# Macaron block on one core: the router's weight travels with the sorted row, GpSimd adds the gathered rows to x

## The chip, the core and the metric

The kernel runs on 1 core of a Trainium2 chip. The metric is the device time of one execution in microseconds. The engines are named as the profile names them: PE (TensorE, matmuls), PEld (its weight loads), DVE (VectorE), ACT (ScalarE), POOL (GpSimd), SP (SyncE, which only issues DMAs here). Each has its own instruction queue and runs it strictly in order; semaphores tie them together.

## The reference

x is 8 batches of 512 tokens by 256 features, f32. Three residual stages:

```python
x = x + 0.5 * ffn(layernorm(x))
x = x + attn(layernorm(x))
x = x + 0.5 * ffn(layernorm(x))
# ffn: probs = softmax(x @ gate_w.T) over 2 experts; sel = argmax; top_w = probs[sel]
#      h = silu(x @ w_gate[sel].T) * (x @ w_up[sel].T); out = top_w * (h @ w_down[sel].T), 1024 wide
# attn: rms_norm, 16 heads of 16, causal softmax, @ Wo, + its own input
```

With two experts the weight of the chosen one is 1 / (1 + exp(-|logit difference|)).

## The kernel before

The FFN is sparse: only the chosen expert is computed for a token. An *item* is one batch of one of the two FFN stages (16 items). The items are grouped into 12 *passes* of one or two items. For an item the kernel takes a layer norm (`l_stats` DVE, `l_rstd` POOL, `l_norm` ACT), splits the normed f32 rows into an f16 high part (`l_split` on ACT, L698, tile xs) and an f16 low part (`l_split` on POOL, L596), takes the logit difference with w_diff (`l_dlogit`, DVE, L881, four reductions, then three small instructions L889 to L892), finds each token's place in the sorted order with small matmuls (`l_prefix`, PE, L1082), writes the place (`l_pos`, DVE, L903), the weight (`l_coef`, DVE, L911 and L912, tile coef), and scatters the rows to DRAM with four indirect DMAs (`l_scatter`, POOL, L609). SP loads them back transposed (`l_load`, L510, tile x_t). A pass then runs 5 or 9 slots of 128 sorted tokens in two units each: gate and up matmuls (L1118 to L1120), `tanh` ACT, `hid` DVE (L926, L930), `h_split` (ACT L717, POOL L650 makes h_lo), down matmuls (L1137 to L1139), `y_out` ACT (L723), `y_store` to y_sorted. `y_gather` (POOL, L623, four indirect DMAs) brings an item's rows back in token order into yt, and `x_update` (DVE, L918, four instructions of 128x256) does x = x + coef * yt.

Between the FFN work runs the attention: 32 *parts* (8 batches, 4 groups of 4 heads), each with scores (PE L1180, L1182; `row_min` on DVE, L983 to L993), the row maximum split into three f16 rows (`max_parts`, DVE, L1003 to L1007) that travel PE, ACT, SP, DRAM and back into extra contraction rows of qt, transposed scores (PE L1197, L1199), exp twice (ACT L786, L787), the low part of the probabilities (`p_lo`, DVE L1012, every fifth one POOL L655), and the product with v (PE L1217). The norm ahead of attention starts with `stats` on DVE (L937), which waits for the batch's x_update.

One list sets the order of everything: `master()` gives every stage a point on one time axis (about 1.2 us a point in the attention stages), sorts by it, and each engine walks the sorted list and issues the stages that concern it. So a stage's number decides what stands in front of it on its engine's queue. Three banks of PSUM (ps_w) go round among scores, transposed scores, projections and transposes: PE can be at most three such tiles ahead of DVE and ACT. `stats` of batch 2 stands one point behind its x_update; for batch 0 also; for the others the distance is 23 points or more.

Of the kernel before, what the change touches and what calls it, by code (L numbers as in the profile page):

```python
# [19 lines left out]
T = S // P  # L20
# [7 lines left out]
MAX_ROWS = 3  # L28
# [100 lines left out]
EXP_LAG = 0.0  # L129
GATHER_LAG = 8  # L130
# [3 lines left out]
               ("l_split", 0, 6.0), ("l_dlogit", 0, 6.5), ("l_exp", 0, 10.5), ("l_prefix", 0, 11.0),  # L134
# [3 lines left out]
            ("l_split", 0): -59.6, ("l_dlogit", 0): -56.5, ("l_exp", 0): -56.4, ("l_prefix", 0): -55.9,  # L138
            ("l_pos", 0): -55.8, ("l_coef", 0): 20, ("l_scatter", 0): -55, ("l_load", 0): -54}
# [101 lines left out]
def macaron(nc, x, rms_w, gate_w, w_gate, w_up, w_down, w_attn, out):  # L241
    with ExitStack() as ctx:  # L242
# [87 lines left out]
        coef = [sb(f"coef{n}", [P, T], F32) for n in range(ROUTES)]  # L330
# [24 lines left out]
        x_sorted = [nc.dram_tensor(f"x_sorted{n}", [PLACES, 2 * D], F16, kind="Internal").ap() for n in range(2)]  # L355
# [120 lines left out]
        def _(sp):  # L476
# [19 lines left out]
            for st in order:  # L496
# [8 lines left out]
                elif what == "l_load":  # L505
# [50 lines left out]
        def _(pool):  # L556
            link = Links(pool, pool_link)
            pool.memset(yt[0][:, 0, :], 0.0).then_inc(zero_ready, 1)
# [22 lines left out]
            for st in order:  # L581
# [11 lines left out]
                elif what == "l_split":  # L593
# [672 lines left out]
```

## Time and profile before

| | us |
|---|---|
| runs: median (lowest to highest, 3 runs) | 1288.9 (1286.12 to 1292.99) |
| the profiled execution's own time | 1289.34 |
| its span, first to last instruction | 1287.6 |
| PE busy | 1091.3 |
| DVE busy | 905.7 |
| ACT busy | 740.2 |
| POOL busy | 531.7 |
| mean granted clock of TensorE | 0.951 |

A busy engine may still wait in places; the share of busy time is a mean over stages. "Idle before" is the time the engine stood still ahead of an instruction, and the releaser named is what ended it.

### The profile page before, as it was taken

The page shows a single profiled execution, that of the slowest core. Times are in us where ns is not written, and L with a number is a line of the kernel's source. Part 1 is how long each engine was busy: PE and PEld are TensorE (multiplying, and loading weights), DVE is VectorE, ACT ScalarE, POOL GpSimd, SP SyncE. Part 2 cuts the span into 40 slices and gives each one's busy share as a digit, 9 for nine tenths or more (in the row PEclk, how much of TensorE's full clock was granted, in tenths as well). Part 3 has the DMA queues.
Part 4 walks back from the last instruction along what each step waited for, and adds up shares of the span by engine and source line. Part 5 has one row for each costly group of instructions (what it writes and reads, how often), then busy time and mean ns, then how long its engine had stood idle before and what let it go on. Part 6 is the DMA issues. An engine that isn't in the chain of part 4 may idle for free. (4 is left out here: it accounts for less than half of the span.)

```text
span 1287.6 us, 39268 instructions
## 1 busy us (share of the span) xinstructions
PE 1091.3 (85%) x14566; PEld 945.8 (73%) x14566; DVE 905.7 (70%) x1912; ACT 740.2 (57%) x1285; POOL 531.7 (41%) x664
## 2 busy tenths in 40 slices
PE   0686888978989898888898799997999989798895
PEld 0576777857778787777777688976877878688784
DVE  6653548796878886978868877887777877874432
ACT  4432425656657665666666566775766756675321
POOL 3146543254523444445234534244452344444432
PEclk9889899998999999999989899998999989998998
DMA  8203231213211122022122141111321012211111
GB/s 315 69 26 83 75 95 49 64 51 80 62 54 34 38 64 87 22 71 76 60 63 73 39 113 44 31 54 41 85 76 57 28 49 61 74 48 47 51 42 46
DMA packets 101326, 83.54 MB, mean 65 GB/s; under 512 B 50240, under 2 KB 95040, under 8 KB 101152
## 3 DMA queue, kind: packets, MB, share of 16 engines
q1 hardware_dynamic: 84064, 54.29, 14.7%
q0 software_dynamic: 6144, 16.79, 4.2%
q10 hardware_dynamic: 10944, 9.97, 2.3%
q8 instruction: 131, 2.15, 0.7%
q14 instruction: 43, 0.35, 0.1%
HBM read 37.36 MB, written 33.69 MB: 55 GB/s over the span
## 5 line engine op out<-in xcount | busy, mean ns | idle before, releaser
L650 POOL TENSOR_TENSOR h_lo<-hid,h_hi 128x256 bf16<-128x256 f32 x304 | 222.5, 753 | 505.1 <-ACT h_hi L717 504.9
L786 ACT ACTIVATE area<-ps_w,s_scale 128x512 f32<-128x512 f32 x320 | 219.6, 686 | 246.6 <-PE ps_w L1199 188.9
L1118 PE MATMUL ps_g<-x_t,w 128*128 128x128 f16 x1096 | 211.8, 227 | 14.9 <-issue 11.4
L787 ACT ACTIVATE area<-ps_w,s_scale 128x512 f16<-128x512 f32 x320 | 217.9, 681 | 0.0
L1120 PE MATMUL ps_g<-x_t,w 128*128 128x128 f16 x1096 | 212.0, 227 | 2.7 <-issue 2.6
L1119 PE MATMUL ps_g<-x_t,w 128*128 128x128 f16 x1096 | 211.2, 226 | 1.9 <-issue 1.9
L1120 PE MATMUL ps_u<-x_t,w 128*128 128x128 f16 x1096 | 210.3, 225 | 1.8 <-issue 1.8
L1118 PE MATMUL ps_u<-x_t,w 128*128 128x128 f16 x1096 | 210.1, 225 | 1.8 <-issue 1.5
L1119 PE MATMUL ps_u<-x_t,w 128*128 128x128 f16 x1096 | 209.2, 224 | 2.4 <-issue 2.3
L1012 DVE TENSOR_TENSOR area<-area 128x512 f16<-128x512 f32 x256 | 193.3, 756 | 14.8 <-ACT area L787 11.1
L1137 PE MATMUL ps_y<-wd,h_hi 128*128 (+1 forms) x608 | 170.8, 281 | 13.7 <-POOL h_lo L650 11.6
L1138 PE MATMUL ps_y<-wd,h_hi 128*128 (+1 forms) x608 | 170.8, 281 | 1.1 <-issue 1.1
L1139 PE MATMUL ps_y<-wd,h_lo 128*128 (+1 forms) x608 | 170.9, 281 | 0.3 <-issue 0.3
L1197 PE MATMUL ps_w<-qt,kt 68*128 68x512 f16 (+3 forms) x512 | 137.3, 306 | 35.6 <-DVE row_min L988 19.0
L1180 PE MATMUL ps_w<-kt,qt 65*128 65x512 f16 (+3 forms) x512 | 138.2, 308 | 13.5 <-DVE row_min L986 8.2
L1118 PEld LDWEIGHTS ps_g<-x_t,w 128*128 (+1 forms) x1096 | 111.2, 101 | 31.7 <-issue 16.8
L711 ACT ACTIVATE hid<-ps_g,g_scale 128x512 f32<-128x512 f32 x137 | 94.2, 688 | 67.1 <-PE ps_g L1120 46.7
L1217 PEld LDWEIGHTS ps_v<-v_parts,area 128*128 128x128 f16 x2560 | 100.7, 97 | 38.7 <-POOL area L655 11.3
L1217 PE MATMUL ps_v<-v_parts,area 128*128 128x33 f16 x2560 | 115.3, 178 | 14.7 <-POOL area L655 10.0
L926 DVE SCALAR_TENSOR_TENSOR hid<-hid,ps_g 128x512 f32<-128x512 f32 x137 | 93.0, 679 | 40.2 <-ACT hid L711 40.0
L717 ACT ACTIVATE h_hi<-hid 128x512 f16<-128x512 f32 x152 | 95.5, 628 | 42.9 <-DVE hid L930 40.1
L1118 PEld LDWEIGHTS ps_u<-x_t,w 128*128 (+1 forms) x1096 | 109.9, 100 | 13.9 <-issue 3.5
(160 smaller groups left out, 2820.0 us busy)
## 6 DMA issues: line engine op xcount, KB each, us to landing
y_sorted<-ys ACTq DMA_DIRECT2D x76, 128.0 KB, 1.7
qk_scratch<-area SPq DMA_DIRECT2D x32, 256.0 KB, 2.2
qt<-qk_scratch SPq DMA_DIRECT2D x128, 64.0 KB, 2.6
kt<-qk_scratch SPq DMA_DIRECT2D x128, 64.0 KB, 2.6
x_buf<-x SPq DMA_DIRECT2D x8, 512.0 KB, 4.2
out<-x_buf SPq DMA_DIRECT2D x8, 512.0 KB, 3.0
x_sorted<-yt SPq DMA_DIRECT2D x18, 128.0 KB, 1.9
area<-w_down SPq DMA_DIRECT2D x4, 512.0 KB, 12.3
```

What stands on the lines that cost most here:

```text
L650: pool.tensor_tensor(h_lo[:, u % 2, c], hid[:, u % 2, c], h_hi[:, u % 2, c], ALU.subtract).then_inc(h_lo_done, 1)
L786: act.activation(p_f32[:, f % 3], ps[:], ACT.Exp, scale=s_scale[:])
L787: act.activation(p_hi[:, f % 4], ps[:], ACT.Exp, scale=s_scale[:]).then_inc(exp_done, 1)
L1012: dve.tensor_tensor(p_lo[:, f % 4], p_f32[:, f % 3], p_hi[:, f % 4], ALU.subtract).then_inc(lo_done, 1)
L1118: pe.matmul(cols, w_hi, x_hi, start=kb == 0 and f == 0, stop=False, skip_group_check=True)
L1119: pe.matmul(cols, w_hi, x_lo, start=False, stop=False, skip_group_check=True)
L1120: ins = pe.matmul(cols, gate_up(u, kind, 1, kb, q * QF + f), x_hi, start=False, stop=kb == KB - 1, skip_group_check=True)
L1137: pe.matmul(ps_y[:, 0:D], hi, wd_lo, start=q == 0 and f == 0, stop=False, skip_group_check=True)
L1138: pe.matmul(ps_y[:, 0:D], hi, wd_hi, start=False, stop=False, skip_group_check=True)
L1139: ins = pe.matmul(ps_y[:, 0:D], lo, wd_hi, start=False, stop=q == 1 and f == QF - 1, skip_group_check=True)
L1180: pe.matmul(ps[:, at:at + keys], qt[0:MAX_AT_ROW, h, i * P:keys], kt[0:MAX_AT_ROW, h, 0:keys], start=n == 0, stop=False, skip_group_check= ...
L1217: ins = pe.matmul(ps_o[n // KINDS % 2][:, hh, i, :], part[:, n % 4, at + (i - j) * P:at + (i - j + 1) * P], v_parts[b % 2][:, j, h, :], st ...
```

## The change

1. The router's weight is no longer applied at x_update. `l_coef` (DVE) writes 1 / (1 + exp) as a 257th column beside the two f16 halves of each row (tile xs_rows, rows of 272 f32, 1088 bytes in place of 1024). The scatter carries it, and so now waits for `l_coef`; `l_coef` of the next item waits for the scatter. SP loads the column back in sorted order after each transposed load (coef_in: 128 x 5 or 128 x 9 elements of 4 bytes), a small POOL instruction per pass multiplies it by the weights' scale (`coef`), and `y_out` on ACT uses it as its per-row scale.
2. `x_update` moves from DVE (four instructions) to POOL (one of 128x1024: x = yt + x).
3. The low part of the rows gets a stage of its own, `l_low`, at point 8.5 of the routing in place of 6.0; `l_dlogit` moves from 6.5 to 6.0.
4. At the start `l_coef` of the first item moves from point 20 to -55.7, `l_dlogit` from -56.5 to -57.5.
5. The row maximum is split into two f16 rows in place of three: two DVE instructions a part in place of four.
6. The first gather no longer waits for the zeroing DMAs, which read a tile of their own.

```diff
-MAX_ROWS = 3
+MAX_ROWS = 2
...
-               ("l_split", 0, 6.0), ("l_dlogit", 0, 6.5), ("l_exp", 0, 10.5), ("l_prefix", 0, 11.0),
+               ("l_split", 0, 6.0), ("l_dlogit", 0, 6.0), ("l_low", 0, 8.5), ("l_exp", 0, 10.5), ("l_prefix", 0, 11.0),
                ("l_pos", 0, 11.2), ("l_coef", 0, 13.0), ("l_scatter", 0, 14.5), ("l_load", 0, 19.0)]
...
         if s == 0 and q == 1:
             put(p, "flags", n)
+            put(p + COEF_LAG, "coef", n)
...
-        xs = sb("xs", [P, T, 2, D], F16)
+        xs_rows = sb("xs_rows", [P, T, XW], F32)
+        xs = xs_rows[:, :, 0:D].bitcast(F16).rearrange("p i (a d) -> p i a d", a=2)
+        xs_coef = xs_rows[:, :, D:D + 1]
...
-        x_sorted = [nc.dram_tensor(f"x_sorted{n}", [PLACES, 2 * D], F16, kind="Internal").ap() for n in range(2)]
+        x_sorted = [nc.dram_tensor(f"x_sorted{n}", [PLACES, XW], F32, kind="Internal").ap() for n in range(2)]
...
+                    if n >= 2:
+                        sp.wait_ge(coef_done, n - 1)
+                    sp.dma_start(coef_in[n % 2][:, 0:SLOTS[n]].unsqueeze(2), x_sorted[n % 2][
+                        0:P * SLOTS[n], D:D + 1].rearrange("(s p) c -> p s c", p=P),
+                        allow_slow_non_contiguous=True).then_inc(coef_loaded[n % 2], 16)
...
-                elif what == "l_split":
+                elif what == "l_low":
                     n = st[1]
                     pool.wait_ge(l_hi, n + 1)
                     pool.tensor_tensor(xs[:, :, 1, :], xn_f[:], xs[:, :, 0, :], ALU.subtract).then_inc(l_lo, 1)
...
                     pool.wait_ge(l_lo, n + 1)
+                    pool.wait_ge(l_coef, n + 1)
...
-                            xs[:, i].rearrange("p a d -> p (a d)"), None).then_inc(scattered, 16)
+                            xs_rows[:, i, :], None).then_inc(scattered, 16)
+                elif what == "x_update":
+                    n = st[1]
+                    b = ITEMS[n][3]
+                    pool.wait_ge(gathered[n % 2], 64 * (n // 2 + 1))
+                    pool.tensor_tensor(x_of(b)[:], yt[n % 2][:], x_of(b)[:], ALU.add).then_inc(x_updated, 1)
+                elif what == "coef":
+                    n = st[1]
+                    pool.wait_ge(coef_loaded[n % 2], 16 * (n // 2 + 1))
...
+                    pool.tensor_scalar(coef[n % 2][:, 0:SLOTS[n]], coef_in[n % 2][:, 0:SLOTS[n]], y_inv[:], None,
+                                       ALU.mult).then_inc(coef_done, 1)
...
-                    act.activation(ys[g % 2][:], ps_y[:, 0:D], ACT.Copy).then_inc(y_copied, 1)
+                    n, s, _ = UNITS[2 * g]
+                    act.wait_ge(coef_done, n + 1)
+                    act.activation(ys[g % 2][:], ps_y[:, 0:D], ACT.Copy, scale=coef[n % 2][:, s:s + 1]).then_inc(y_copied, 1)
...
-                    link(dve.tensor_scalar(prob[:], e_abs[:], 1.0, y_scale[:], ALU.add, ALU.mult))
-                    link(dve.reciprocal(coef[r][:], prob[:]))
-                elif what == "x_update":
...
-                    for i in range(T):
-                        ins = dve.scalar_tensor_tensor(out=x_of(b)[:, i, :], in0=yt[n % 2][:, i, :],
-                                                       scalar=coef[n % ROUTES][:, i:i + 1], in1=x_of(b)[:, i, :],
-                                                       op0=ALU.mult, op1=ALU.add)
-                    ins.then_inc(x_updated, 1)
+                    if n:
+                        dve.wait_ge(scattered, 64 * n)
+                    link(dve.tensor_scalar(prob[:], e_abs[:], 1.0, None, ALU.add))
+                    dve.reciprocal(xs_coef, prob[:].unsqueeze(2)).then_inc(l_coef, 1)
...
                     link(dve.tensor_scalar(part[0], minima, -1.0 / MAX_SCALE, None, ALU.mult))
-                    link(dve.scalar_tensor_tensor(out=max_rest[:], in0=minima, scalar=-1.0 / MAX_SCALE, in1=part[0],
-                                                  op0=ALU.mult, op1=ALU.subtract))
-                    link(dve.tensor_copy(part[1], max_rest[:]))
-                    dve.tensor_tensor(part[2], max_rest[:], part[1],
-                                      ALU.subtract).then_inc(max_parts_done, 1)
+                    dve.scalar_tensor_tensor(out=part[1], in0=minima, scalar=-1.0 / MAX_SCALE, in1=part[0],
+                                             op0=ALU.mult, op1=ALU.subtract).then_inc(max_parts_done, 1)
```


POOL, the routing of an item at 436 to 444 us in the trace before (xs and xs_rows are the low part, area is p_lo). Before:

```order
L592 TENSOR_TENSOR l_shift<-l_scale,l_minus_mean 128x4
L655 TENSOR_TENSOR area<-area 128x512
L650 TENSOR_TENSOR h_lo<-hid,h_hi 128x256 x2
L596 TENSOR_TENSOR xs<-xn_f,xs 128x4x256
L650 TENSOR_TENSOR h_lo<-hid,h_hi 128x256 x2
L655 TENSOR_TENSOR area<-area 128x512
L650 TENSOR_TENSOR h_lo<-hid,h_hi 128x256 x2
```

After:

```order
L606 TENSOR_TENSOR l_shift<-l_scale,l_minus_mean 128x4
L681 TENSOR_TENSOR area<-area 128x512
L676 TENSOR_TENSOR h_lo<-hid,h_hi 128x256 x4
L610 TENSOR_TENSOR xs_rows<-xn_f,xs_rows 128x4x256
L681 TENSOR_TENSOR area<-area 128x512
L676 TENSOR_TENSOR h_lo<-hid,h_hi 128x256 x2
```

The low part stands behind two more h_lo instructions.

POOL, the gathers and updates of batches 2 and 3 (yt and x_buf; tmp_pool is the first instruction of `rstd`, behind `stats`). Before:

```order
L623 DMA yt<-y_sorted,place 128x256 x4
L650 TENSOR_TENSOR h_lo<-hid,h_hi 128x256 x2
L623 DMA yt<-y_sorted,place 128x256 x4
L655 TENSOR_TENSOR area<-area 128x512
L631 TENSOR_SCALAR tmp_pool<-mean_var 128x4
```

After:

```order
L649 DMA yt<-y_sorted,place 128x256 x4
L676 TENSOR_TENSOR h_lo<-hid,h_hi 128x256 x2
L649 DMA yt<-y_sorted,place 128x256 x4
L681 TENSOR_TENSOR area<-area 128x512
L631 TENSOR_TENSOR x_buf<-yt,x_buf 128x1024
L657 TENSOR_SCALAR tmp_pool<-mean_var 128x4
```

The update of batch 2 stands behind the gather of batch 3 and a p_lo.

DVE at the start, from the logit difference to the placing of the first item. Before:

```order
L881 ISA dlogit 128x1
L889 TENSOR_SCALAR sel<-dlogit 128x4
L890 SCALAR_TENSOR_TENSOR high_place<-dlogit,from_top 128x4
L892 SCALAR_TENSOR_TENSOR neg_abs<-dlogit 128x4
L801 TENSOR_REDUCE w_max<-qt 128x1
L903 TENSOR_TENSOR place<-high_place,ps_w 128x4
L905 CAST low_count<-ps_w 1x1
L801 TENSOR_REDUCE w_max<-kt 128x1 x4
```

After:

```order
L909 ISA dlogit 128x1
L917 TENSOR_SCALAR sel<-dlogit 128x4
L918 SCALAR_TENSOR_TENSOR high_place<-dlogit,from_top 128x4
L920 SCALAR_TENSOR_TENSOR neg_abs<-dlogit 128x4
L829 TENSOR_REDUCE w_max<-qt 128x1 x2
L931 TENSOR_TENSOR place<-high_place,ps_w 128x4
L933 CAST low_count<-ps_w 1x1
L940 TENSOR_SCALAR prob<-e_abs 128x4
L941 RECIPROCAL xs_rows<-prob 128x4
L829 TENSOR_REDUCE w_max<-kt 128x1 x4
```

One more reduction of the weights (w_max) stands ahead of place, and prob and the reciprocal, for which the scatter now waits, right behind low_count.

## Rows read from the trace of the kernel before

**Rows 1.** the page, its span and the busy time of each engine

```profile
span 1287.6 us, 39268 instructions
PE 1091.3 (85%) x14566; PEld 945.8 (73%) x14566; DVE 905.7 (70%) x1912; ACT 740.2 (57%) x1285; POOL 531.7 (41%) x664
```

**Rows 2.** windows view, attention stages; columns: stretch, length, busy of each, PEclk, DMA, GB/s

```profile
190.00:1180.00 990.00, 881.51 (x12079) 761.34 (x12080) 769.20 (x1614) 640.14 (x1121) 410.50 (x495) 0.96 0.20 58
```

**Rows 3.** timeline of PE: start, length, instruction, [idle before and its releaser]

```profile
446.44 0.40 PE L1197 MATMUL ps_w<-qt,kt 68*128 68x256 f16 x1 [3.76 <-DVE row_min L988]
...
1205.14 0.17 PE L1082 MATMUL ps_w<-sel,upper 128*128 128x5 bf16 x1 [1.97 <-DVE neg_abs L892]
```

**Rows 4.** timeline of DVE and POOL before the first of these gaps

```profile
441.10 0.42 DVE L881 CUSTOM_DVE_ANT_0 junk<-xn_f,w_diff 128x256 bf16<-128x256 f32 x1
...
441.57 2.27 DVE L881 CUSTOM_DVE_ANT_0 junk<-xn_f,w_diff 128x256 bf16<-128x256 f32 x1
...
445.70 0.69 DVE L988 TENSOR_REDUCE row_min<-ps_w 128x4 f32<-128x512 f32 x1
...
441.43 2.13 POOL L596 TENSOR_TENSOR xs<-xn_f,xs 128x1024 f16<-128x1024 f32 x1 [1.96 <-ACT xs L698]
```

**Rows 5.** windows view around the first of these gaps

```profile
444.00:446.00 2.00, 0.00 (x0) 0.00 (x0) 1.97 (x7) 0.00 (x0) 0.99 (x2) 0.69 0.42 114
446.00:448.00 2.00, 1.56 (x13) 1.44 (x14) 2.00 (x4) 0.70 (x2) 0.00 (x0) 0.50 0.18 51
```

**Rows 6.** timeline of DVE at another item, 271 us

```profile
270.97 2.09 DVE L1012 TENSOR_TENSOR area<-area 128x512 f16<-128x512 f32 x1
```

**Rows 7.** groups of instructions: line, count, busy us, mean ns, idle before

```profile
L918 DVE SCALAR_TENSOR_TENSOR x_buf<-yt,coef,x_buf 128x256 f32<-128x256 f32 x64 | 30.4, 536 | 17.6 <-DMA yt<-y_sorted,place 17.6
L1006 DVE CAST max_parts<-max_rest 128x16 f16<-128x16 f32 x32 | 9.6, 301 | 1.1
L1007 DVE TENSOR_TENSOR max_parts<-max_rest,max_parts 128x16 f16<-128x16 f32 x32 | 6.5, 204 | 1.1
L596 POOL TENSOR_TENSOR xs<-xn_f,xs 128x1024 f16<-128x1024 f32 x16 | 35.8, 2239 | 32.4 <-ACT xs L698 32.4
```

**Rows 8.** windows view, 10 us stretches with DVE nearly full and PE not

```profile
270.00:280.00 10.00, 6.35 (x87) 5.00 (x84) 9.83 (x25) 5.87 (x11) 4.20 (x5) 1.00 0.04 14
...
1120.00:1130.00 10.00, 6.28 (x80) 5.62 (x78) 9.09 (x21) 5.71 (x11) 4.38 (x5) 0.87 0.01 3
```

**Rows 9.** timelines of POOL, DVE and PE, the update of batch 2 and its norm

```profile
348.70 1.17 POOL L655 TENSOR_TENSOR area<-area 128x512 f16<-128x512 f32 x1
...
348.94 0.75 DVE L937 BATCH_NORM_STATS2 bn<-x_buf 128x6 f32<-128x256 f32 x2
...
350.34 0.23 PE L1180 MATMUL ps_w<-kt,qt 65*128 65x128 f16 x1 [1.75 <-DVE row_min L986]
```

**Rows 10.** timelines of DVE, POOL, SP and PE, the first routing at the start

```profile
17.39 1.21 DVE L801 TENSOR_REDUCE w_max<-qt 128x1 f32<-128x1024 f32 x1
...
19.03 1.23 POOL L609 DMA_INDIRECT x_sorted<-xs,place  x1 [2.65 <-DVE low_count L905]
...
29.18 2.78 SPq L510 DMA_TRANSPOSE x_t<-x_sorted  x1
...
34.10 0.27 PE L1118 MATMUL ps_g<-x_t,w 128*128 128x128 f16 x1 [8.62 <-issue]
```

**Rows 11.** timeline of PE, a wait behind four scatters on POOL

```profile
556.98 0.29 PE L1217 MATMUL ps_v<-v_parts,area 128*128 128x33 f16 x5 [3.48 <-POOL area L655]
```

**Rows 12.** the chain that ended last, its end: start, length, what

```profile
1282.13 0.48 DVE x_buf L918
...
1283.01 0.79 DVE x_buf L918 x2
```

**Rows 13.** the page, DMA queues: packets, MB, share of 16 engines

```profile
q1 hardware_dynamic: 84064, 54.29, 14.7%
q0 software_dynamic: 6144, 16.79, 4.2%
```

More of the change, by code:

```diff
@@ L59 @@
 XSCALE = 2.0**11
+XW = D + 16
 H_SCALE = 2.0**-54
@@ L129 @@
 EXP_LAG = 0.0
+COEF_LAG = 1.0
 GATHER_LAG = 8
@@ L133 @@
 ROUTE_STEPS = [("l_stats", 0, 0.0), ("l_stats", 1, 0.5), ("l_rstd", 0, 1.5), ("l_norm", 0, 4.0),
-               ("l_split", 0, 6.0), ("l_dlogit", 0, 6.5), ("l_exp", 0, 10.5), ("l_prefix", 0, 11.0),
+               ("l_split", 0, 6.0), ("l_dlogit", 0, 6.0), ("l_low", 0, 8.5), ("l_exp", 0, 10.5), ("l_prefix", 0, 11.0),
                ("l_pos", 0, 11.2), ("l_coef", 0, 13.0), ("l_scatter", 0, 14.5), ("l_load", 0, 19.0)]
 START_AT = {("l_stats", 0): -60, ("l_stats", 1): -59.9, ("l_rstd", 0): -59.8, ("l_norm", 0): -59.7,
-            ("l_split", 0): -59.6, ("l_dlogit", 0): -56.5, ("l_exp", 0): -56.4, ("l_prefix", 0): -55.9,
-            ("l_pos", 0): -55.8, ("l_coef", 0): 20, ("l_scatter", 0): -55, ("l_load", 0): -54}
+            ("l_split", 0): -59.6, ("l_dlogit", 0): -57.5, ("l_low", 0): -56.5, ("l_exp", 0): -56.4, ("l_prefix", 0): -55.9,
+            ("l_pos", 0): -55.8, ("l_coef", 0): -55.7, ("l_scatter", 0): -55, ("l_load", 0): -54}
 MAX_AT = [-59, -58, -57, -56, -55, -54, -53, -52, -51.2, -51, -46.8, -46.6]
@@ L267, in macaron @@
         yt = [sb(f"yt{n}", [P, T, D], F32) for n in range(2)]
+        zeros = sb("zeros", [P, XW], F32)
         xt_hi = sb("xt_hi", [P, KB, S], F32R)
@@ L329, in macaron @@
         place = [sb(f"place{n}", [P, T], I32) for n in range(ROUTES)]
-        coef = [sb(f"coef{n}", [P, T], F32) for n in range(ROUTES)]
+        coef_in = [sb(f"coef_in{n}", [P, MAX_SLOTS], F32) for n in range(2)]
+        coef = [sb(f"coef{n}", [P, MAX_SLOTS], F32) for n in range(2)]
         low_count = [sb(f"low_count{n}", [1, 1], I32) for n in range(3)]
@@ L382, in macaron @@
         down_done, y_copied, x_updated = sem("down_done"), sem("y_copied"), sem("x_updated")
+        l_coef, coef_loaded, coef_done, y_inv_done = sem("l_coef"), sems("coef_loaded", 2), sem("coef_done"), sem("y_inv_done")
         proj_done, part1_done, part2_done = sem("proj_done"), sem("part1_done"), sem("part2_done")
@@ L618, in _ @@
                         pool.wait_ge(x_updated, n - 1)
-                    elif n == 0:
-                        for parity in range(2):
-                            pool.wait_ge(zeroed[parity], 16 * MAX_SLOTS)
                     for i in range(T):
@@ L1001, in _ @@
                     minima = row_min[:, p % 2, :, 0, :]
-                    part = [max_parts[:, r].rearrange("p (h i) -> p h i", i=T) for r in range(3)]
+                    part = [max_parts[:, r].rearrange("p (h i) -> p h i", i=T) for r in range(MAX_ROWS)]
                     link(dve.tensor_scalar(part[0], minima, -1.0 / MAX_SCALE, None, ALU.mult))
-                    link(dve.scalar_tensor_tensor(out=max_rest[:], in0=minima, scalar=-1.0 / MAX_SCALE, in1=part[0],
-                                                  op0=ALU.mult, op1=ALU.subtract))
-                    link(dve.tensor_copy(part[1], max_rest[:]))
-                    dve.tensor_tensor(part[2], max_rest[:], part[1],
-                                      ALU.subtract).then_inc(max_parts_done, 1)
+                    dve.scalar_tensor_tensor(out=part[1], in0=minima, scalar=-1.0 / MAX_SCALE, in1=part[0],
+                                             op0=ALU.mult, op1=ALU.subtract).then_inc(max_parts_done, 1)
                 elif what == "p_lo" and st[2] % KINDS < KINDS - 1:
```

22 lines of the change are left out of this document (11 added, 11 removed).

## The prediction, made before the changed kernel ran

> **What bounds the kernel now.** I read the page's busy times first: PE 1091.3 us of a span of 1287.6 [rows 1]. So PE is the bound on the whole, and an instruction taken from another engine is worth something only where PE stands still for it. The windows view of the attention stages (190 to 1180 us) says how much that is at most: PE 881.5 of 990 us, so 108 us idle, at a granted clock of 0.96, while DVE is busy 769.2 us and POOL 410.5 us [rows 2]. Then I went through the timeline of PE for its gaps. The long ones have one pattern. At 446.44 us PE has waited 3.76 us for a row_min of DVE [rows 3]. DVE was late because one of the four reductions of `l_dlogit` took 2.27 us where its neighbour took 0.42 us; it started at 441.57, and POOL had started the low part of the rows (L596, 2.13 us) at 441.43 and held it until that ended [rows 4]. Five gaps of 3.3 to 4.2 us inside the attention stages and one of 1.97 us at 1205 us stand behind such a pair, 20.7 us together (the first and the last of the six are shown) [rows 3]. Each long one costs again behind itself: the granted clock of TensorE falls to 0.69 in the stretch of the gap and is 0.50 (1.2 GHz in place of 2.4) in the next, where PE works again [rows 5]. At items where the low part misses `l_dlogit`, it holds a p_lo of DVE instead: 2.09 us for one L1012 [rows 6].
>
> **A: the low part moves from point 6.0 to 8.5, the logit difference from 6.5 to 6.0.** The low part then stands behind two more h_lo on POOL, some 3 us later, when the reductions are over. At each of the six places DVE gets 2.27 - 0.42 = 1.85 us back [rows 4]. It doesn't keep all: the low part still takes 2.13 us, and while DVE is saturated some L1012 will run into it, up to 2.09 - 0.68 = 1.4 us, where 0.68 is the plain length of the row_min beside it (0.69 in [rows 4]; L1012 has the same shape). I take half of that, 0.7 us. So 6 x 1.15 = 6.9 us. Bounds: 0 (every collision only moves) and 6 x 1.85 = 11.1 us. If gaps of nearly 4 us become gaps of 2, less of the half-clock time follows. One such tail costs about 2 us (2 us at 0.50 shown, about twice that long each time); for five long gaps I take half, 5 us; bounds 0 and 10.
>
> **B: two DVE instructions fewer in `max_parts`.** 9.6 + 6.5 + 2.2 us of idle between them = 18.3 us of DVE over 32 parts [rows 7].
>
> **C: x_update leaves DVE.** It frees 30.4 us [rows 7], and puts 16 POOL instructions of 128x1024 in its place. No row shows this add; the nearest is the low part of the same length, 2.239 us mean [rows 7] and 2.13 us unhindered [rows 4]. I take 2.13, with 1.67 (what DVE takes for it [rows 12]) and twice 2.13 as ends, since both inputs are now f32. Each reads SBUF beside p_lo on DVE, so it can hold an L1012 as the low part does: up to 1.4 us, or nothing. For 13 updates inside the attention stages at the upper end that is 18 us given back, so B and C free 31 to 49 us of DVE, say 36.
> How much of B and C reaches PE? Of the 99 stretches of 10 us between 190 and 1180 us, 14 have DVE at 9.0 us or more and PE below 10 (the first and the last are shown) [rows 8]. Elsewhere freed DVE time is hidden by PE itself. 36 x 14/99 = 5.1 us; bounds 0 and a third, 12 us.
> The trace gives the collision first: a DVE instruction that reads two tiles in SBUF waits out a POOL tensor_tensor [rows 4, 6], while the hid and row_min instructions, which read PSUM, don't show it.
> The Trainium skill says the same of it in "SBUF — State Buffer", section "Who interferes with whom": DVE and GpSimd share a pair of ports by an exclusive lock, and the second one to issue blocks fully, also for a DVE instruction with two SBUF inputs against a GpSimd read. By that rule this change hands DVE 16 more locks, and a saturated DVE would gain nothing from C; this is what the rival "the collisions only move" is made of. "GPSIMD Engine Reference", section "Elementwise — side-by-side cycle accounting", has 4497 ns for an f32 add of 2048 columns; an estimate from it is 2.25 us for 1024, and no row here shows this add.
>
> **D: costs.**
> Start: place now stands behind one more w_max (1.21 us at 17.39), and prob and the reciprocal (about 0.4 us) behind it, ahead of the scatter that starts at 19.03; the reductions start some 0.4 us earlier. From there the chain is scatter, transposed load at 29.18, first gate matmul at 34.10 [rows 10]. The DMA engines are full of weights then, which may hide it. +1.2 us, bounds 0 and +1.7.
> Batch 2: `stats` starts at 348.94 on DVE, but POOL is at its gather and p_lo until 348.70 + 1.17 = 349.87, and only then comes the update: 352.0 [rows 9]. `stats` waits 3.1 us, and row_min, for which PE already stood 1.75 us [rows 9], waits behind it. The 1.7 us that DVE no longer spends just before are mostly lost to waiting. +2.5 us, bounds 0 and +5.
> POOL queue: after the double passes (4 times) the update stands right behind four gather DMAs, with h_lo and p_lo behind it. PE has waited 3.48 us for a p_lo behind four scatters [rows 11], so there is no slack there. Between +0 and 4 x 2.13 = 8.5 us; I take +1.2, as only a p_lo or h_lo due in just that stretch counts.
> End: the last update is on the chain that ends last, 1282.13 to 1283.80 us on DVE, 1.67 us [rows 12]; on POOL 2.13: +0.5.
> At nothing I cost: `y_out` with a scale per row (0 to +0.1 us each, ACT has slack); the scatter's wait for l_coef later on (l_coef stands 1.5 points ahead); 6% longer rows; the smaller row maximum on PE, ACT and SP; the 12 loads of coef_in, 9728 elements of 4 bytes. For these no row exists. By the mean of a packet, 14.7% x 16 x 1287.6 / 84064 = 36 ns on q1 and 4.2% x 16 x 1287.6 / 6144 = 141 ns on q0 [rows 13], the 72 per engine of the largest load take 2.6 to 10 us. They are wanted some 20 points after they are issued, but the row maximum's two DMAs stand behind them on SP's queue.
>
> **Sum.** -6.9 - 5 - 5.1 + 1.2 + 2.5 + 1.2 + 0.5 = -11.6. On the profiled execution's 1289.34 us (its span 1287.6 and 1.7 around it; the median of the runs, 1288.9, is within 0.4 of it) this gives 1277.7, so 1278 us.
>
> **Rivals.**
> *The collisions only move.* The low part and the update catch an L1012 each time, at 1.4 us; A gives 0 and the clock still falls, and B and C together give 5.1 against costs of 5.4: 1289 - 1290 us. For it: rows 6, and that POOL always finds a saturated DVE at these places. Against it: the worst gaps are those where `l_dlogit` was hit, not an L1012.
> *POOL's queue becomes what PE waits for.* Place: each gather of an attention item, then the wait for its landing, then the update, with p_lo and h_lo behind. From the point where a p_lo is due within 2 us after the update starts, PE pays 2.13 us. At 12 items 25.6 us less the gains of 17: 1289.3 + 5.4 + 25.6 - 17 = 1303 if all pay, 1297 at three quarters. For it: rows 11. Against it: POOL is busy 410 of 990 us, and the update stands 8 points, about 10 us, behind its gather, by when most gathers have landed.
> *The small loads hold up the row maximum.* If a coef_in load takes 10 us, the row maximum's round trip behind it on SP and the DMA rings is late at the six passes where it follows within 6 points: about 3 us each with nothing else lost, 18 us: 1296 us.
> *The gaps go altogether.* 1.85 us at six places, all 10 us of slow clock, 12 of B and C: -33 + 5: about 1262.
>
> **Chances.** Forecast (1271 to 1284) 0.48; collisions only move 0.23; POOL's queue 0.14; small loads 0.05; the gaps go 0.10. What a measurement can tell from no change is about 0.5%, 6.4 us. Faster by more than that: 0.43 of the forecast and all of the last, 0.53; within: 0.05 and 0.22, 0.27; slower: 0.14 + 0.05 + 0.01 = 0.20. The cases have both signs, so the range reaches from 1264 to 1297; the forecast's own is 1271 to 1284.
>
> **What would show it.** A: the longest reduction of `l_dlogit` near 0.42 us, PE's gaps behind it near 2 us, the clock above 0.5 there. Collisions moved: L1012 with a higher mean and as many of 2 us. B: max_parts two rows shorter. C: the POOL add at 2.1 us; `stats` of batch 2 waiting for POOL by 3 us. Start: the first gate matmul 1 us later. POOL rival: PE waiting for h_lo or area of POOL by 20 us more in total. Small loads: coef_in landing late and PE waiting for max_scratch. The forecast is wrong if PE's idle time inside 190 to 1180 us doesn't fall by at least 5 us, or its clock there not rise.

## The result, and the profile after

| | before | after |
|---|---|---|
| median, us (lowest to highest, 4 runs each) | 1290.45 (1286.12 to 1292.99) | 1255.34 (1253.81 to 1261.15) |
| ratio, 95% interval | | 0.974, 0.9697 to 0.9782 |
| span of the profiled execution | 1287.6 | 1254.2 |
| PE busy / not busy in the span | 1091.3 / 196.3 | 1078.9 / 175.3 |
| DVE, POOL busy | 905.7, 531.7 | 860.2, 571.8 |
| mean granted clock | 0.951 | 0.963 |

The change is faster by 2.6%, 35 us of medians. I had forecast 1278 us with a range down to 1264, so the sign was right and the size was a third of the measured one. Of the 33.4 us between the two spans 21.0 are idle time of PE. The other 12.4 are busy time for the same number of matmuls (14566), with the mean granted clock at 0.963 in place of 0.951. The page after:

```profile
span 1254.2 us, 39207 instructions
PE 1078.9 (86%) x14566; PEld 933.9 (74%) x14566; DVE 860.2 (69%) x1784; ACT 744.7 (59%) x1285; POOL 571.8 (46%) x693
```

The windows view of the attention stages (columns as in [rows 2]):

```profile
190.00:1180.00 990.00, 901.08 (x12482) 779.02 (x12481) 745.39 (x1538) 655.39 (x1142) 457.70 (x536) 0.97 0.21 59
```

Set against [rows 1] and [rows 2], PE is busy 20 us more in the same 990 us, with DVE 24 us less busy and POOL 47 us more. The other groups of the change, from the lines view (line, form, count, busy us and mean ns, idle before):

```profile
L631 POOL TENSOR_TENSOR x_buf<-yt,x_buf 128x1024 f32<-128x1024 f32 x16 | 37.7, 2357 | 3.4 <-DMA yt<-y_sorted,place 3.3
...
L909 DVE CUSTOM_DVE_ANT_0 junk<-xn_f,w_diff 128x256 bf16<-128x256 f32 x64 | 33.9, 530 | 9.9 <-ACT xn_f L716 8.2
...
L1029 DVE TENSOR_TENSOR area<-area 128x512 f16<-128x512 f32 x256 | 206.6, 807 | 18.9 <-ACT area L815 15.4 <-issue 3.5
```

The add takes 2.357 us (I took 2.13, with the bounds 1.67 and 4.26). The estimate of 2.25 us for it, half of what the Trainium skill's "GPSIMD Engine Reference", section "Elementwise — side-by-side cycle accounting", has for an f32 add of 2048 columns, is 5% below the measured time.

The p_lo group (L1029, L1012 before) went *up* from 193.3 us (mean 756 ns) to 206.6 (807). The chain of `l_dlogit` (four reductions, sel, high_place, neg_abs) went down: against 0.42, 0.17 and 0.15 us for one of each unhindered, it lost 25.0 us over the 16 items before and 9.7 after. So most of DVE's waiting for POOL is still there, only on another instruction. PE's gap of [rows 3] that ended at 446.44 ends at 444.68 now. The timelines of PE, DVE and POOL there:

```profile
444.68 0.28 PE L1214 MATMUL ps_w<-qt,kt 67*128 67x256 f16 x1 [2.13 <-DVE row_min L1008]
...
442.02 0.42 DVE L909 CUSTOM_DVE_ANT_0 junk<-xn_f,w_diff 128x256 bf16<-128x256 f32 x1
...
443.94 0.68 DVE L1008 TENSOR_REDUCE row_min<-ps_w 128x4 f32<-128x512 f32 x1
444.55 2.63 DVE L1029 TENSOR_TENSOR area<-area 128x512 f16<-128x512 f32 x1
...
444.51 2.12 POOL L610 TENSOR_TENSOR xs_rows<-xn_f,xs_rows 128x1024 f16<-128x1024 f32 x1
```

The low part (L610) still holds DVE for 2 us, but now a p_lo behind the row_min for which PE waits, not a reduction ahead of it. The clock in the windows there (the stretches of [rows 5] read 0.69 and 0.50):

```profile
444.00:446.00 2.00, 1.32 (x19) 1.21 (x19) 2.00 (x3) 0.77 (x2) 2.00 (x2) 1.00 0.43 130
446.00:448.00 2.00, 1.31 (x18) 1.01 (x17) 2.00 (x3) 1.17 (x3) 2.00 (x2) 1.00 0.21 67
```

Where the 33 us come from shows in the start times of y_out (76 of them in the same order in both), before minus after. Steps elsewhere are smaller than 4 us and partly cancel:

| y_out | before | after | difference | what lies since the row above |
|---|---|---|---|---|
| 25th | 434.21 | 434.34 | -0.13 | start; batch 2 |
| 26th | 455.40 | 452.71 | 2.69 | gap of 446 us |
| 36th | 639.22 | 634.10 | 5.12 | gap of 519 us (2.11) |
| 39th | 697.91 | 685.50 | 12.41 | gap of 643 us |
| 49th | 877.61 | 863.38 | 14.23 | |
| 50th | 903.60 | 886.68 | 16.92 | gap of 895 us |
| 57th | 1017.78 | 1000.40 | 17.38 | |
| 59th | 1050.92 | 1028.36 | 22.56 | gap of 1044 us |
| 63rd | 1114.65 | 1088.92 | 25.73 | |
| 64th | 1135.75 | 1107.88 | 27.87 | gap of 1128 us |
| 67th | 1175.05 | 1145.19 | 29.86 | |
| 70th | 1214.43 | 1178.58 | 35.85 | gap of 1205 us |
| 76th | 1272.86 | 1238.86 | 34.00 | end |

The six steps with a collision gap are 2.8, 7.3, 2.7, 5.2, 2.1 and 6.0: 26 us of 33 (whatever else happened between two y_out is in them too). Six collisions were the right place to look; I had 11.9 us for them.

### The profile page after: what moved, and what is told of

It reads as the page before. It is cut to its first block and busy times, and to the rows that moved or that the text cites. A ratio compares the mean times of both kernels' runs of the same rounds, so it can differ in the third digit from the quotient of the medians.

```text
span 1254.2 us, 39207 instructions
## 1 busy us (share of the span) xinstructions
PE 1078.9 (86%) x14566; PEld 933.9 (74%) x14566; DVE 860.2 (69%) x1784; ACT 744.7 (59%) x1285; POOL 571.8 (46%) x693
## 5 line engine op out<-in xcount | busy, mean ns | idle before, releaser
L676 POOL TENSOR_TENSOR h_lo<-hid,h_hi 128x256 bf16<-128x256 f32 x304 | 217.7, 737 | 480.9 <-ACT h_hi L743 479.9
L1029 DVE TENSOR_TENSOR area<-area 128x512 f16<-128x512 f32 x256 | 206.6, 807 | 18.9 <-ACT area L815 15.4
L1135 PE MATMUL ps_u<-x_t,w 128*128 128x128 f16 x1096 | 205.6, 222 | 2.9 <-issue 2.7
L1137 PE MATMUL ps_u<-x_t,w 128*128 128x128 f16 x1096 | 205.8, 222 | 1.7 <-issue 1.5
L1136 PE MATMUL ps_u<-x_t,w 128*128 128x128 f16 x1096 | 204.5, 221 | 1.8 <-issue 1.8
L1154 PE MATMUL ps_y<-wd,h_hi 128*128 (+1 forms) x608 | 169.1, 278 | 14.8 <-POOL h_lo L676 12.1
L1155 PE MATMUL ps_y<-wd,h_hi 128*128 (+1 forms) x608 | 169.0, 278 | 0.1
L1214 PE MATMUL ps_w<-qt,kt 67*128 67x512 f16 (+3 forms) x512 | 135.9, 304 | 17.4 <-DVE row_min L1008 7.3
L1006 DVE TENSOR_REDUCE row_min<-ps_w 128x1 f32<-128x512 f32 x128 | 87.6, 684 | 48.3 <-PE ps_w L1199 37.0
```

Source lines behind the costliest of these rows:

```text
L676: pool.tensor_tensor(h_lo[:, u % 2, c], hid[:, u % 2, c], h_hi[:, u % 2, c], ALU.subtract).then_inc(h_lo_done, 1)
L1029: dve.tensor_tensor(p_lo[:, f % 4], p_f32[:, f % 3], p_hi[:, f % 4], ALU.subtract).then_inc(lo_done, 1)
L1135: pe.matmul(cols, w_hi, x_hi, start=kb == 0 and f == 0, stop=False, skip_group_check=True)
L1136: pe.matmul(cols, w_hi, x_lo, start=False, stop=False, skip_group_check=True)
L1137: ins = pe.matmul(cols, gate_up(u, kind, 1, kb, q * QF + f), x_hi, start=False, stop=kb == KB - 1, skip_group_check=True)
L1154: pe.matmul(ps_y[:, 0:D], hi, wd_lo, start=q == 0 and f == 0, stop=False, skip_group_check=True)
```

## The experiments

Theory 1: what the change brings is that the low part no longer delays the instructions between two row_min, by PE's gap and by the slow clock behind it. Theory 2, the rival: it is DVE's relief (x_update, the row maximum). The kernels were timed in five comparisons of two to four, each on one chip together with the kernel before, whose median lay between 1262 and 1293 us in them. So ratios to the kernel before are compared, with 95% intervals, and medians only within one comparison. Where an expectation has only microseconds, they were written for a kernel before of 1290 us, and are read here as a share of that.

**The points alone** (on the kernel before, the start as it was):

```diff
-("l_split", 0, 6.0), ("l_dlogit", 0, 6.5),
+("l_split", 0, 6.0), ("l_dlogit", 0, 6.0), ("l_low", 0, 8.5),
```

> The kernel before with one edit: the low part of the rows gets its own stage at point 8.5, and l_dlogit goes from 6.5 to 6.0 (the first item as before). Theory 1 (the gain is the collision of the low part with l_dlogit: once DVE is 1.85 us earlier, PE's gaps of 3.3 to 4.2 us shrink to 2 or less, and a gap of that size costs no slow clock): five or six of the long gaps go, 13 us of idle time and 12 to 15 us of slow clock, so 1261 to 1268 us, and the clock from 0.951 to about 0.96. Theory 2 (the gain is DVE's relief by x_update and the row maximum; by the points alone the low part only catches an L1012 in place of l_dlogit, as my rival said): 1284 to 1292 us, long gaps of PE as many as before at other places.

Measured: 0.9812 (0.9784 to 0.984), 1261.25 against 1283.95 us, in theory 1's range (0.977 to 0.983). Two numbers in a table bring 1.9% of the change's 2.6%; in its later timings below the change brings 2.2 and 2.4%. The one gap of over 1.5 us for a row_min left at the six places is 1.56 us at 641. DVE's busy time fell by only 4.1 us in it:

```profile
PE 1085.1 (86%) x14566; PEld 940.3 (75%) x14566; DVE 901.6 (71%) x1912; ACT 739.9 (59%) x1285; POOL 534.2 (42%) x664
```

**Which of the two points.** One kernel with the low part at 8.5 alone (l_dlogit left at 6.5), one with l_dlogit at 6.0 alone (the low part left at 6.0), in one comparison:

> The kernel before with one edit: the low part at point 8.5 in place of 6.0; l_dlogit stays at 6.5. Theory 1 (the whole gain of the points is that the low part no longer starts while the reductions run): 0.979 to 0.985 of before, as with both points moved. Theory 2 (half of it is that l_dlogit, half a point sooner, stands ahead of another row_min): 0.988 to 0.994.

> The kernel before with the other edit: l_dlogit at point 6.0 in place of 6.5, the low part at 6.0 as before. Theory 1: the low part still meets the reductions or the three small instructions behind them, so 0.995 to 1.003. Theory 2: 0.988 to 0.994.

Measured: 0.9802 (0.9782 to 0.9821) and 0.9999 (0.9976 to 1.0022). The low part's place is all of it. From 183 us on the two run alike up to the place at 446 us, so they show it best. With l_dlogit sooner alone, the timelines of DVE, POOL and PE:

```profile
440.54 2.27 DVE L881 CUSTOM_DVE_ANT_0 junk<-xn_f,w_diff 128x256 bf16<-128x256 f32 x1
...
442.85 0.51 DVE L889 TENSOR_SCALAR sel<-dlogit 128x4 bf16<-128x4 f32 x1
443.27 0.15 DVE L890 SCALAR_TENSOR_TENSOR high_place<-dlogit,from_top 128x4 f32<-128x4 f32 x1
443.34 0.63 DVE L892 SCALAR_TENSOR_TENSOR neg_abs<-dlogit 128x4 f32<-128x4 f32 x1
...
444.67 0.69 DVE L988 TENSOR_REDUCE row_min<-ps_w 128x4 f32<-128x512 f32 x1
...
440.40 2.12 POOL L596 TENSOR_TENSOR xs<-xn_f,xs 128x1024 f16<-128x1024 f32 x1 [1.97 <-ACT xs L698]
442.49 1.47 POOL L650 TENSOR_TENSOR h_lo<-hid,h_hi 128x256 bf16<-128x256 f32 x2
...
445.41 0.39 PE L1197 MATMUL ps_w<-qt,kt 68*128 68x256 f16 x1 [3.77 <-DVE row_min L988]
```

With the low part later alone, the same place:

```profile
440.52 0.42 DVE L881 CUSTOM_DVE_ANT_0 junk<-xn_f,w_diff 128x256 bf16<-128x256 f32 x1
...
440.98 0.17 DVE L889 TENSOR_SCALAR sel<-dlogit 128x4 bf16<-128x4 f32 x1
441.06 0.15 DVE L890 SCALAR_TENSOR_TENSOR high_place<-dlogit,from_top 128x4 f32<-128x4 f32 x1
441.13 0.15 DVE L892 SCALAR_TENSOR_TENSOR neg_abs<-dlogit 128x4 f32<-128x4 f32 x1
...
441.98 0.68 DVE L988 TENSOR_REDUCE row_min<-ps_w 128x4 f32<-128x512 f32 x1
...
443.78 2.65 DVE L1012 TENSOR_TENSOR area<-area 128x512 f16<-128x512 f32 x1
...
443.76 2.12 POOL L596 TENSOR_TENSOR xs<-xn_f,xs 128x1024 f16<-128x1024 f32 x1
...
442.72 0.28 PE L1197 MATMUL ps_w<-qt,kt 68*128 68x256 f16 x1 [1.10 <-DVE row_min L988]
```

The row_min comes 2.69 us sooner: 1.85 from the reduction, 0.34 from sel (0.51 against 0.17) and 0.48 from neg_abs (0.63 against 0.15), both slow while POOL ran the two h_lo behind the low part (442.49 to 443.96); the rest is rounding. PE's gap shrinks by the same 2.67 us. The p_lo that the low part now catches takes 2.65 us, and no gap of PE follows it. The windows view of both, 2 us each from 444 (first with l_dlogit sooner alone, then with the low part later alone):

```profile
444.00:446.00 2.00, 0.59 (x4) 0.47 (x5) 1.97 (x6) 0.00 (x0) 0.00 (x0) 0.50 0.48 137
446.00:448.00 2.00, 2.00 (x21) 2.00 (x20) 1.15 (x2) 1.72 (x3) 0.39 (x1) 0.50 0.01 3
```

```profile
444.00:446.00 2.00, 2.00 (x36) 1.72 (x36) 2.00 (x1) 1.21 (x3) 2.00 (x2) 1.00 0.35 101
446.00:448.00 2.00, 2.00 (x29) 1.65 (x27) 1.97 (x6) 1.26 (x2) 1.44 (x1) 1.00 0.00 0
```

At 0.50 PE gets 21 matmuls into 2 us, at 1.00 some 29 to 36. Over the whole kernel the two spans are 1261.8 and 1239.2 us: 8.9 us of the 22.6 are busy time of PE (1081.3 and 1072.4), the rest is idle time. In the start times of y_out the six places bring 4.5, 4.5, 1.3, 3.5, 3.5 and 3.5 us, 20.8 of the 22.6.

**The old points in the changed kernel**, low part at 6.0 and l_dlogit at 6.5:

```diff
-("l_dlogit", 0, 6.0), ("l_low", 0, 8.5),
+("l_low", 0, 6.0), ("l_dlogit", 0, 6.5),
```

> The changed kernel with the low part back at point 6.0 and l_dlogit at 6.5, beside each other as before (the first item stays as changed). Theory 1: the collisions are back, and with them the gaps over 3 us and the slow clock behind them, less what two DVE instructions fewer take off: 1275 to 1285 us. Theory 2: little is lost, 1256 to 1262 us.

Measured: 0.9925 (0.9902 to 0.9948), 1273.84 us. Theory 1 again (0.988 to 0.996): without the points the change keeps 0.75% of its 2.6%. The gap of 3.76 us is 4.33 in it (at 446.75), and the clock behind it is at 0.50 again.

**The rest alone: two rows for the maximum** (on the kernel before):

```diff
-MAX_ROWS = 3
+MAX_ROWS = 2
```

and the two DVE instructions behind it left out, as in the change.

> The kernel before with one edit: the row maximum in two f16 rows, two DVE instructions a part fewer (the lower digits of the maximum are left out, as in the changed kernel). 18 us of DVE time go, spread over 32 parts. Theory 1: the collisions stay, so the long gaps stay, each 0.6 us shorter at most; 1284 to 1290 us. Theory 2 (DVE's relief is the gain): a third or more of the 33 us, 1272 to 1280 us.

Measured: 0.9948 (0.9925 to 0.9971), 1279.33 us. A real 0.5%, at the lower end of theory 1's range (0.995 to 1.000) and less than theory 2 wants (0.986 to 0.992). The microseconds alone would have said theory 2, as the kernel before took only 1283.95 us here.

**The points and the two rows together** (timed twice):

> The kernel before with two edits: the points of the low part and l_dlogit, and the row maximum in two f16 rows. The points alone gave 0.981 of before, the two rows alone 0.995. Theory 1 (the parts add up, each takes its own piece of PE's idle and slow-clock time): 0.976, about 1253 to 1260 us, so that nothing is left for x_update's move and the weight on the row. Theory 2 (the remaining gaps are no longer DVE's, so two rows bring nothing more): 0.981, 1261 us.

> The kernel before with the points and the two-row maximum, beside the changed kernel. Theory 1 (the two rows add their 0.5% to the points): 0.974 to 0.978, level with the changed kernel, so that the weight on the row and x_update on POOL are worth nothing together. Theory 2 (two rows add little once the collisions are gone): 0.979 to 0.982, 4 to 8 us slower than the changed kernel.

Measured: 0.9792 (0.975 to 0.9834) and 0.9797 (0.9778 to 0.9816). They do not add up to 0.976, so theory 2 holds in both: once the collisions are gone, two rows bring 0.1 or 0.2% against the points alone, which is less than the intervals.

**x_update on DVE in the changed kernel** (also twice):

```diff
-pool.tensor_tensor(x_of(b)[:], yt[n % 2][:], x_of(b)[:], ALU.add)
+for i in range(T):
+    dve.scalar_tensor_tensor(out=x_of(b)[:, i, :], in0=yt[n % 2][:, i, :], scalar=1.0, in1=x_of(b)[:, i, :], op0=ALU.mult, op1=ALU.add)
```

> The changed kernel with x_update on DVE again, four instructions of 128x256 an item as before (x = 1.0 * yt + x, the weight stays in y_out). Theory 1: moving x_update brings little, as DVE's relief there is hidden by PE and the add on POOL costs a p_lo now and then; 1253 to 1260 us, and the wait of batch 2's stats for POOL (5.6 us of PE at 355 us) is gone. Theory 2: DVE is the scarce engine, 30 us more on it bring back a third of the gain: 1264 to 1272 us.

> The changed kernel with x_update on DVE in four instructions, on the same chip as the changed kernel this time. Theory 1 (30 us less on DVE is worth something to PE even though the add holds a p_lo on POOL's side): 0.978 to 0.982 of before, 4 to 8 us slower than the changed kernel. Theory 2 (it is hidden both ways): within 2 us of it.

The changed kernel as it is, in the second and the fourth comparison:

> The changed kernel as it is, as the measure for the others on the same chip: 0.974 of before by its first timing, between 0.970 and 0.978.

> The changed kernel as it is, as the measure for the others of this job: 0.974 to 0.976 of before.

Measured: 0.9792 (0.9765 to 0.9819) and 0.9802 (0.9777 to 0.9826) for x_update on DVE; 0.9761 (0.9722 to 0.9799) and 0.9779 (0.9753 to 0.9804) for the changed kernel. In the fourth comparison, which had all of them, the medians are 1233.5 (changed), 1237.5 (x_update on DVE) and 1237.3 us (points and rows alone), with intervals that overlap. That is the lower end of theory 1 for x_update on DVE, and theory 2 for points and rows. The wait of batch 2's stats is gone in the trace with x_update on DVE, as expected, and the kernel was no faster for it. The three differences to the changed kernel within one comparison have the same sign, 0.2 or 0.3%, and each alone is inside its intervals. So x_update on POOL and the weight on the row are worth between nothing and 0.5%. The sum had B and C at 5.1 us against 5.4 of costs, about nothing; that is not refuted.

**The wait of batch 2.** The gather of batch 3 moved behind the norm of batch 2:

```diff
-put(end + GATHER_LAG, "y_gather", k)
+put(245.6 if k == 3 else end + GATHER_LAG, "y_gather", k)
-put(at, "x_update", k)
+put(253 if k == 3 else at, "x_update", k)
```

> The changed kernel with the gather of batch 3 moved from point 241.2 to 245.6, behind the update and the norm of batch 2, and its update from 249.2 to 253. POOL then adds batch 2 some 5 us sooner, and stats no longer waits 5.17 us on DVE. Theory 1 (that wait is what PE's gap of 5.6 us at 355 us and the 3.4 us of slow clock behind it are made of): both go, but as the trace of the changed kernel had 4.3 us of it back 10 us later, 3 to 6 us faster than the changed kernel, 1249 to 1252 us at its clock. Theory 2 (the lost time is given back anyway by queues that run ahead): within 2 us of it.

Measured: 0.9738 (0.9696 to 0.9781), 1260.69 against 1261.69 us for the changed kernel, as theory 2 had it. The place is mended: in the changed kernel stats waited 5.17 us and PE 5.60 us,

```profile
354.05 0.75 DVE L957 BATCH_NORM_STATS2 bn<-x_buf 128x6 f32<-128x256 f32 x2 [5.17 <-POOL x_buf L631]
...
355.44 0.29 PE L1197 MATMUL ps_w<-kt,qt 65*128 65x128 f16 x1 [5.60 <-DVE row_min L1006]
```

and in this kernel 0.35 and 0.79 us:

```profile
347.16 0.75 DVE L957 BATCH_NORM_STATS2 bn<-x_buf 128x6 f32<-128x256 f32 x2 [0.35 <-POOL x_buf L631]
...
348.56 0.23 PE L1197 MATMUL ps_w<-kt,qt 65*128 65x128 f16 x1 [0.79 <-DVE row_min L1006]
```

Its y_out starts are 6.8 us ahead of the first trace after at 396 us, 2.4 at 1000, and 4.8 behind at the end; the mean clock is 0.956 against 0.963. Whether that is given back by rule or by the luck of where the clock falls, one trace can't say. With l_dlogit at 6.5 as well:

> The changed kernel with two edits: the gather of batch 3 moved behind the norm of batch 2, and l_dlogit at point 6.5 again (the low part stays at 8.5). Theory 1 (both mended places count in the end): 3 to 6 us faster than the changed kernel on this chip. Theory 2 (time mended there is given back later by the queues and the clock): within 2 us of it.

Measured: 0.9787 (0.9759 to 0.9814), 1232.84 against 1233.52 us for the changed kernel: nothing, theory 2 again. I found no version that beats the changed kernel by more than the measurement can tell.

**The low part cut** to 16 of 256 columns, in the changed kernel (the memset that zeroes the rest is wider too):

```diff
-xs[:, :, 1, :], xn_f[:], xs[:, :, 0, :], ALU.subtract
+xs[:, :, 1, 0:16], xn_f[:, :, 0:16], xs[:, :, 0, 0:16], ALU.subtract
```

> The changed kernel with the low part cut to 16 of 256 columns (the low digits of the rest of the normed rows are left out, zero in their place), so that POOL holds no port for 2.1 us any more. Theory 1 (at point 8.5 the low part's collision falls on a p_lo, whose reader on PE stands three fills behind, and costs next to nothing): 0.971 to 0.977, within 3 us of the changed kernel. Theory 2 (each of the 16 still costs PE about a microsecond, the gain was only the difference between two places): 0.960 to 0.967, 10 to 18 us faster than the changed kernel.

Measured: 0.9735 (0.9713 to 0.9757), theory 1. This comparison had no changed kernel in it; against its 0.974, 0.9761 and 0.9779 of the others it is 0.05 to 0.4%, where theory 2 wanted 1% and more. By these ratios the 16 low parts of 2.1 us cost some 6 us together at most at point 8.5.

**l_dlogit in halves**, two reductions at 5.0 and two at 7.2, with the late gather of batch 3 (not shown in the cut):

```diff
+("l_dlogit", 0, 5.0),
 ("l_split", 0, 6.0),
-("l_dlogit", 0, 6.0),
+("l_dlogit", 1, 7.2),
 ("l_low", 0, 8.5),
```

> The changed kernel with the gather of batch 3 behind the norm of batch 2, and l_dlogit in two halves, two reductions at point 5.0 and two with the three small instructions at 7.2, so that a row_min stands between them. Theory 1 (what is left of PE's gaps at the routing, 2.1 us at 444 and 1100 us and 1.6 at 635 us, is DVE's chain of four reductions itself): they go, 4 to 8 us faster than the changed kernel, about 0.970 of before. Theory 2 (gaps of 2 us or less cost little, as no slow clock stands behind them, and the second half meets the low part again): within 0.3% of the changed kernel, 0.973 to 0.977, or slower.

Measured: 0.9898 (0.9877 to 0.9918), 1.2 to 1.6% slower than the changed kernel in its three timings. Theory 1's number is a miss; theory 2 had the cause, in its last words. Its timeline of DVE tells why:

```profile
431.84 0.43 DVE L909 CUSTOM_DVE_ANT_0 junk<-xn_f,w_diff 128x256 bf16<-128x256 f32 x1 [2.85 <-ACT xn_f L716]
...
437.84 2.08 DVE L922 SCALAR_TENSOR_TENSOR neg_abs<-dlogit 128x4 f32<-128x4 f32 x1
439.85 0.68 DVE L1010 TENSOR_REDUCE row_min<-ps_w 128x4 f32<-128x512 f32 x1
```

The first half stands too early and waits for xn_f (25.2 us of DVE in all, 8.2 in the changed kernel), and the second half is late enough that the low part catches neg_abs ahead of the row_min: the old collision, and PE's gap before the next matmul is 3.85 us.

**A delay by DVE's own work**: each reduction done twice, on the kernel with the points, and again with the low part at 10.5 beside its own control.

```diff
-for i in range(T):
+for i in 2 * list(range(T)):
```

> The kernel before with the points moved, so that the low part no longer meets the reductions, and each of the four reductions of l_dlogit done twice, which makes DVE late by about 2 us at the same place with no help from POOL. Theory 1 (what costs is DVE's lateness there, by the gap of PE that it makes and the slow clock behind it, whoever caused it): the gaps over 3 us at the six places come back, 0.995 to 1.003 of before, 1280 to 1290 us. Theory 2 (the low part at point 6.0 costs in some other way, for instance by holding POOL or by the time at which the scatter gets its rows): the time stays near 0.981 to 0.986, 1261 to 1267 us, as DVE has time to spare.

> The kernel before with l_dlogit at 6.0 and the low part at 10.5 (8.5 in the changed kernel). Theory 1 (any place clear of the reductions will do, the scatter at 14.5 leaves slack): 0.978 to 0.984 of before. Theory 2 (a later low part makes the scatter and x_t late): 0.984 to 0.992.

> The same with each of the four reductions done twice, 4 x 0.46 = 1.9 us more on DVE an item and no collision there. Theory 1 (lateness of DVE ahead of a row_min is what costs, by whomever): at 14 items some 1.9 to 3.5 us each, the clock included, so 27 to 49 us above the run beside it, 1.000 to 1.018 of before. Theory 2 (only the collision with POOL costs, DVE's own work of that length is absorbed): within 10 us of it, 0.978 to 0.988.

Measured: 1.0182 (1.0141 to 1.0223); then 0.9819 (0.979 to 0.9848) for the control and 1.0203 (1.0171 to 1.0234) with the delay. Both delays cost more than theory 1 had (up to 1.003 and 1.018), and neither is the clean test that I wanted. In the last one, at 458 us, POOL still comes to the low part as the chain ends, right behind the same h_lo as at point 8.5:

```profile
458.40 2.08 DVE L892 SCALAR_TENSOR_TENSOR neg_abs<-dlogit 128x4 f32<-128x4 f32 x1
...
461.92 0.39 PE L1197 MATMUL ps_w<-qt,kt 68*128 68x256 f16 x1 [5.59 <-DVE row_min L988]
```

What they show is a price for both together: 35 us more of DVE (937.1 against 901.8 busy, stalls included) cost 50 us of time. How much of it is the collision and how much the doubled work is not shown, so that lateness of DVE costs the same whoever makes it stays an argument. The control says little of its own: in its trace, too, the low part stands right behind the same h_lo (443.26 us, and 443.76 with the low part at 8.5 alone).

## Why the prediction was wrong

**What bounds, and where.** Right, with one misreading. The six places are where the gain is, 26 of 33 us, and the points alone give 0.980 to 0.981. But the held instruction was a reduction at five of them only. At 895 us the last reduction had started before the low part and ran its 0.42 us, and sel behind it was held:

```profile
890.95 2.27 POOL L596 TENSOR_TENSOR xs<-xn_f,xs 128x1024 f16<-128x1024 f32 x1 [3.20 <-ACT xs L698]
...
891.28 1.97 DVE L889 TENSOR_SCALAR sel<-dlogit 128x4 bf16<-128x4 f32 x1
```

**A, the size of the stall: wrong, and this is the term that failed, with its clock.** I had 6 x 1.15 = 6.9 us of gap and 5 us of clock, 11.9; the points alone gave about 23 us (1283.95 to 1261.25), and the low part's point alone 25 (1262.18 to 1237.52). Three steps in it:
- The stall at the place compared is 2.69 us and not 1.85. I counted the reduction and not sel and neg_abs behind it, which were slow beside h_lo. In the trace of before the whole chain is 2.68, 2.64, 2.29, 3.46, 2.69 and 2.64 us longer than unhindered at the six places, 16.4 us, where even my upper bound was 11.1. In the trace after it is 0.2 us.
- "While DVE is saturated some L1012 will run into it", for which I took off 0.7 us a place: it does run into one, and longer than I had it (2.63 and 2.65 us). But no gap of PE follows it: the matmul that reads it (pv) stands three fills later in the list (`PV_LAG` is 3; a fill is one tile of transposed scores). I priced the collision by DVE's time and not by who waits. DVE's busy time hardly fell in the points' run (4.1 us for 23 us of time).
- The clock. I took 2 us for a tail and half of the tails. The trace of before has 1.7 or 3.4 us of full-clock work in each stretch at the lower level, and at the six places 15.3 us together, of which some 2 fall in time that PE still stood idle. In the trace after the clock stays at 1.00 at five of the six. This part is luck in some measure: in the other two traces of the same kernel it stays so at four and at three of them. The upper bounds of A, 11.1 and 10, nearly held the points' 23 us; the forecast sat between them and a lower end that rested on the p_lo for which nobody waits.

**B and C.** I had 5.1 us. Two rows alone 0.5%, with the points 0.1 or 0.2%; x_update on POOL and the weight on the row 0 to 0.5%. That is within the bounds (0 to 12), and too small here to say more of the share of saturated stretches as a guide. What the change has beyond the points, 0.2 to 0.7% or 3 to 9 us, no experiment splits further.

**D.** Start: +1.2 expected, the first y_out is 1.58 us later, and the lead is back by the third. Batch 2: stats waits 5.17 us, not 3.1, and PE 5.60; the start of exp is 5.6 us late at 362 us and 1.3 at 373, so most of it comes back, and with the wait gone (the late gather) the kernel was 1 us faster. The +2.5 can't be called wrong as a cost. POOL's queue after double passes: the gaps for p_lo were there before and are alike ([rows 11] has 3.48 us, the trace after 3.57 at 552.82). End: +0.5, and the last chain ends with an update of 2.34 us against 1.67.

**The rivals.** *The collisions only move*: true as an event and false as a cost, the most useful error here. Its sign, L1012 with a higher mean, came (756 to 807 ns) together with the forecast's signs for A, so it could not tell the two apart; PE's gaps could. I had built it on the rule of the Trainium skill, "SBUF — State Buffer", section "Who interferes with whom", by which the pair of ports that DVE and GpSimd share is an exclusive lock, and a DVE instruction with two inputs in SBUF contends with a GpSimd instruction that reads SBUF. The trace agrees: p_lo, started 0.02 us after a low part of 2.12 us, took 2.65 us and not 0.68. Which of DVE's instructions can bear the wait, only the order of this kernel says.

*POOL's queue* didn't come: PE waited 21.6 us for h_lo and area of POOL before and 22.3 after, where 20 us more was the sign. Nor did *the small loads*: coef_in lands in 3.0 us (2.4 to 6.3), where I had 2.6 to 10.

```profile
L521 SPq DMA_DIRECT2D coef_in<-x_sorted x12: 563/582/588, 33.3 to 1185.8; - x12
...
DMA to landing us min/median/max: 2.4/3.0/6.3
```

*The gaps go altogether* (1262 us, chance 0.10) was the nearest, and is still 7 us above the measured time, as it too had 1.85 us a place and 10 us of clock.

## What to carry to other kernels

Where two engines block each other, a shift of one stage may only move the collision, as it did here, so put it where the blocked instruction has its reader far behind: moving one stage by 2.5 points was worth 2%, freeing 30 us of the same engine next to nothing. Price a stall by the wait at the bounding engine with all that stands between the stall and the release, and add the slow clock behind each gap of 3 us or more as a full piece (1.7 or 3.4 us here). A shift of such a stage is cheap to try in both directions, and its place should be checked in the trace of every new order, as two of my own edits moved the collision back ahead of the row_min.

## What the runs showed of the hardware

- The granted clock often falls behind a gap of PE. In the 20 traces of this case, between 100 and 1225 us, 179 of 183 gaps of 3 us or more end within 2 us of a stretch at the lower level (0.50), which then costs 2.75 us of full-clock work in the mean (mostly 1.7 or 3.4 us). Of gaps of 2 to 3 us 84 of 111 do, of gaps of 1.5 to 2 us 35 of 125; a moment picked at random does in 13% of the time. The same kernel differs from run to run: in the three traces of the changed kernel none of 4, 4 of 7 and 5 of 6 gaps of 2 to 3 us have one. So the expectation that a gap of 2 us costs no slow clock was wrong.
- POOL's low part holds small DVE instructions as fully as large ones: neg_abs of 128x4, 0.15 us alone, took 2.08 us (with l_dlogit in halves, and with the delay), and sel of 128x4, 0.17 us alone, took 1.97 us (at 891 us in the trace before).
- The kernel before had medians of 1290, 1284, 1293, 1262, 1262 and 1285 us in six comparisons on several chips, and the changed kernel's ratio to it stayed at 0.974 to 0.978 in the three that it was in.
